# Stacking the queries of the first eight heads by selecting matmuls in place of a trip through DRAM

## The reference

```python
Q = proj(q, Wq, bq); K = proj(k, Wk, bk); V = proj(v, Wv, bv)   # (B, 16, S, 16)
loc_s = einsum('bhnqd,bhnkd->bhnqk', Qb, Kb) * scale            # a block's own 128 keys
out = einsum('bhnqk,bhnkd->bhnqd', softmax(loc_s), Vb)
cross_s = einsum('bhnqd,bhnkd->bhnqk', Qb, Kw) * scale          # keys of blocks n-1, n, n+1
cross_s = where(kmask, cross_s, -inf)
out = out + einsum('bhnqk,bhnkd->bhnqd', softmax(cross_s), Vw)
```

## Time and profile before

| | |
|---|---|
| timed runs, median (lowest to highest) | 917.14 us (916.61 to 918.33) |
| profiled execution, its own time | 918.54 us |
| its span | 916.8 us |
| mean granted clock of PE | 0.926 of full speed |
| PE busy | 820.7 us (90%) |
| DVE, ACT, POOL busy | 401.9, 345.8, 242.9 us |

### The profile page before, as it was taken

The page is one execution under the profiler, slowest core; times in us unless marked ns, Lnnn a source line. Parts: engine busy times, 40 slices in busy tenths (PEclk is TensorE's granted clock), DMA queues, the critical chain, the costliest instruction groups (busy, mean ns, idle before and its releaser), DMA issues. The chain is left out here.

```text
span 916.8 us, 15571 instructions
## 1 busy us (share of the span) xinstructions
PE 820.7 (90%) x5010; PEld 620.5 (68%) x5011; DVE 401.9 (44%) x746; ACT 345.8 (38%) x898; POOL 242.9 (26%) x258
## 2 busy tenths in 40 slices
PE   5689999999999999999399998999999999999930
PEld 4567776767586757757399995766666777666620
DVE  5636585686457644633465542222211222222116
ACT  1121455354434542452354430333333333333313
POOL 5912111141113101200417774111111111111116
PEclk9987999999589957999799999999999999999985
DMA  9952324506050444000561117431111110110034
GB/s 299 173 161 64 56 86 103 96 1 171 16 93 2 113 142 72 1 4 1 193 234 53 58 58 203 133 125 35 29 34 34 34 34 29 34 34 29 23 115 177
DMA packets 56981, 76.83 MB, mean 84 GB/s; under 512 B 15888, under 2 KB 41360, under 8 KB 56048
## 3 DMA queue, kind: packets, MB, share of 16 engines
q1 hardware_dynamic: 53536, 66.99, 27.4%
q0 software_dynamic: 3408, 9.34, 2.9%
HBM read 50.82 MB, written 24.98 MB: 83 GB/s over the span
## 5 line engine op out<-in xcount | busy, mean ns | idle before, releaser
L1678 PE MATMUL ps<-we,xT 128*128 x312 | 142.3, 599 | 1.9 <-issue 1.9
L1698 PE MATMUL ps<-we,hT 128*128 x624 | 141.1, 379 | 2.5 <-ACT hT L794 2.5
L1698 PEld LDWEIGHTS ps<-we,hT 128*128 128x128 f32 x624 | 118.5, 190 | 35.0 <-issue 20.9
L1022 DVE TENSOR_REDUCE mx<-ps 128x4 f32<-128x512 f32 (+1 forms) x128 | 104.1, 821 | 79.4 <-PE ps L1510 77.7
L1226 DVE COPY hp<-ps 128x512 f32<-128x512 f32 x78 | 50.3, 686 | 160.1 <-PE ps L1678 160.1
L794 ACT ACTIVATE hT<-ps,b1T 128x128 f32<-128x128 f32 x312 | 84.7, 382 | 37.2 <-PE ps L1689 37.2
L1678 PEld LDWEIGHTS ps<-we,xT 128*128 128x128 f32 x312 | 56.7, 192 | 59.0 <-issue 58.9
L1510 PE MATMUL ps<-k_stack,q_stack 96*128 96x256 f32 (+1 forms) x256 | 81.9, 410 | 8.2 <-DMA q_stack<-q_rows 5.9
L696 ACT ACTIVATE pT<-ps 128x256 f32<-128x256 f32 x128 | 49.1, 384 | 103.1 <-PE ps L1526 96.3
L590 ACT ACTIVATE xT<-ps 128x256 f32<-128x256 f32 x39 | 14.8, 383 | 180.8 <-PE ps L1661 180.8
L1510 PEld LDWEIGHTS ps<-k_stack,q_stack 96*128 96x128 f32 x256 | 46.0, 224 | 43.9 <-issue 23.8
(11 more groups left out here) (214 smaller groups left out, 1238.2 us busy)
## 6 DMA issues: line engine op xcount, KB each, us to landing
we<-in_w SPq DMA_DIRECT2D x16, 1024.0 KB
k_stack<-k_rows SPq DMA_DIRECT2D x24, 256.0 KB, 4.8
q_stack<-q_rows SPq DMA_DIRECT2D x96, 64.0 KB, 4.8
slot_rows<-attn SPq DMA_DIRECT2D x1, 4992.0 KB, 24.8
xs<-slot_rows SPq DMA_DIRECT2D x39, 128.0 KB, 2.1
k_rows<-k_s SPq DMA_DIRECT2D x16, 256.0 KB, 2.5
q_rows<-q_s SPq DMA_DIRECT2D x16, 256.0 KB, 3.4
yl<-pair_out SPq DMA_DIRECT2D x4, 1024.0 KB, 9.4
```

Source lines behind the costliest of these rows:

```text
L1022: nc.vector.tensor_reduce(mx[:, n, 2 * p:2 * p + 2, r0:r0 + nb], ps[:, 2 * (u % 2):2 * (u % 2) + 2, 0:nb * P].rearrange("p h (b k) -> p h ...
L1678: m = nc.tensor.matmul(ps[:, 2 + c, :], xT[:, q, k, :], w[:, bass.ds(e, 1), k * HID + c * 512:k * HID + (c + 1) * 512].rearrange("p o n -> ...
L1698: m = nc.tensor.matmul(ps[:, 6, 0:D], hT[:, c, :], w[:, bass.ds(e, 1), KD * HID + c * D:KD * HID + (c + 1) * D].rearrange("p o n -> p (o n)"),
```

## The change

The queries of heads 0 to 7 no longer go through DRAM. PE multiplies `q_s[:, 0]` by a selecting matrix `sel` (`q_s` times ones and zeros), two matmuls (high and low part) for each of four pairs of heads, which puts the 96 stacked rows of a pair into PSUM bank `p`. ScalarE (pairs 0 and 2) and VectorE (pairs 1 and 3) copy each bank twice into `q_stack`, once multiplied by `parity[:, 0]` and once by `parity[:, 1]`, per-partition factors of 1 and 0 that clear the other head of the pair. Keys, and queries of heads 8 to 15, go through DRAM as before. The eight matmuls stand ahead of the value matmuls and wait for `cb_out`; the six fillers are gone, while batch 0 keeps its 24 (in bank 5). POOL builds `sel` near its start, VectorE `parity`.

```diff
+        sel = W_s[0][:, 3, :, :, :].rearrange("p l k n -> p (l k n)")[:, 0:PAIRS * 160].rearrange("p (g c) -> p g c", g=PAIRS)
+        parity = sb("parity", [P, 2], F, att)
@@ POOL, behind mask_s
+            nc.gpsimd.memset(sel.bitcast(F), 0.0).then_inc(s["sel_set"], 1)
+            pool.wait_ge(s["sel_set"], 1)
+            for at in (0, 32, 128):
+                nc.gpsimd.tensor_copy(sel[:, :, at:at + 32], ident[:, :].rearrange("p (c g) -> p g c", g=PAIRS))\
+                    .then_inc(s["sel_set"], 1)
@@ ACT, project2, behind projected(3)
+                for p in (0, 2):
+                    act.wait_ge(s["sel_ps"], PAIRS * b + p + 1)
+                    for par in range(2):
+                        last = nc.scalar.activation(q_stack[0:STACK, PAIRS * par + p, :], ps[0:STACK, p, :], ACT.Copy,
+                                                    scale=parity[0:STACK, par:par + 1])
+                    last.then_inc(s["sel_act"], 1)
@@ DVE, start
+            dve.wait_ge(s["consts"], 5)
+            nc.vector.tensor_reduce(parity[:, :], ident[:, :].rearrange("p (k a r) -> p a k r", a=2, r=DH), AXY, ALU.max)\
+                .then_inc(s["parity_set"], 1)
@@ DVE, project2, behind projected(3)
+                for p in (1, 3):
+                    dve.wait_ge(s["sel_ps"], PAIRS * b + p + 1)
+                    for par in range(2):
+                        last = nc.vector.tensor_scalar(q_stack[0:STACK, PAIRS * par + p, :], ps[0:STACK, p, :],
+                                                       parity[0:STACK, par:par + 1], None, ALU.mult)
+                    last.then_inc(s["sel_dve"], 1)
@@ PE, project2
                 projected(3)
+                if c is None:
+                    pe.wait_ge(s["sel_set"], 4)
+                    pe.wait_ge(s["masks"], 1)
+                else:
+                    pe.wait_ge(s["cb_out"], c + 1)
+                pe.wait_ge(s["qk2_lo"], 4 * b + 2)
+                for p in range(PAIRS):
+                    for l in range(2):
+                        m = nc.tensor.matmul(ps[0:STACK, p, :], sel[:, p, 64 * l:64 * l + STACK], q_s[:, 0, l, :],
+                                             start=l == 0, stop=l == 1)
+                    m.then_inc(s["sel_ps"], 1)
                 for i in range(2):
                     pe.wait_ge(s["qk2_lo"], 4 * b + 1 + 2 * i)
                     rows_of(6, c_s, w, 2, "v2_ps", i)
-                if c is not None:
-                    pe.wait_ge(s["cb_out"], c + 1)
-                keep_clock(WARM if c is None else WARM_Q, bank=0)
                 pe.wait_ge(s["qk2_lo"], 4 * b + 4)
+                if c is None:
+                    keep_clock(WARM, bank=5)
@@ PE, half
                         if u == 0:
-                            pe.wait_ge(stacked[ha], 16 * STACK_DMAS * (b + 1))
-                        if u == UNITS // 2:
-                            pe.wait_ge(stacked_late[ha], 16 * LATE_DMAS * (b + 1))
+                            pe.wait_ge(stacked[ha], 16 * (KEY_DMAS + (LATE_DMAS if ha else 0)) * (b + 1))
+                        if ha and u == UNITS // 2:
+                            pe.wait_ge(stacked_late, 16 * LATE_DMAS * (b + 1))
+                        if not ha and u < 2:
+                            pe.wait_ge(s["sel_act"], 2 * b + u + 1)
+                            pe.wait_ge(s["sel_dve"], 2 * b + u + 1)
@@ SP, body of a batch (queries of half 0 and their aways are gone)
                 stack_keys(b, 0)
-                stack_queries(b, 0)
-                rows_away(b, 1, k_rows, k_s, k_away, 1)
-                rows_away(b, 1, q_rows, q_s, q_away, 2)
+                keys_away(b, 1)
+                queries_away(b)
```

More of the change, by code:

```diff
@@ L27 @@
 AX = mybir.AxisListType.X
+AXY = mybir.AxisListType.XY
 P = 128
@@ L55 @@
 WARM = 24
-WARM_Q = 6
 WARM_B = 16
@@ L62 @@
 PAIRS = HALF // 2
-STACK_DMAS = 3 + 2 * 3
+KEY_DMAS = 3
 LATE_DMAS = 2 * 3
+STACK = 96
 def side_blocks(i):
@@ L84, in build @@
         k_rows = nc.dram_tensor("k_rows", (2, 2, P, S), F, kind="Internal").ap()
-        q_rows = nc.dram_tensor("q_rows", (2, 2, P, S), F, kind="Internal").ap()
+        q_rows = nc.dram_tensor("q_rows", (2, P, S), F, kind="Internal").ap()
         pair_out = nc.dram_tensor("pair_out", (2 * T + SLOTS, D), F, kind="Internal").ap()
@@ L213, in build @@
           a_ps a_red aug_step aug_ready augT_ps augT_out b_ps b_exp pv_done oc_out os_out
+          sel_set parity_set sel_ps sel_act sel_dve
           cb_ps w_exp cb_step cb_out v2_ps v2_out at_ps at_hi at_lo w2_ps
@@ L223, in build @@
                                             for n in ("xs_in", "yw_sent", "st_step", "st_sent"))
-        k_away, q_away = ([sem(f"s_{n}_away{h}_{part}") for h in range(2) for part in ("hi", "lo")] for n in "kq")
-        stacked, stacked_late = ([sem(f"s_{n}{h}") for h in range(2)] for n in ("stacked", "stacked_late"))
+        k_away = [sem(f"s_k_away{h}_{part}") for h in range(2) for part in ("hi", "lo")]
+        q_away = [sem(f"s_q_away_{part}") for part in ("hi", "lo")]
+        stacked = [sem(f"s_stacked{h}") for h in range(2)]
+        stacked_late = sem("s_stacked_late")
         yl_in = [sem(f"s_yl_in{b}") for b in range(B)]
@@ L258, in _, with keys_away, queries_away @@
             sp.dma_start(slot_rows[:, D:].rearrange("(i p) d -> p i d", p=P), pad_end[:, :, :]).then_inc(s["pad_out"], 16)
-            def rows_away(b, h, rows, src, away, j):
+            def keys_away(b, h):
                 for part, ready in enumerate(("qk2_hi", "qk2_lo")):
-                    sp.wait_ge(s[ready], 4 * b + 2 * h + j)
-                    sp.dma_start(rows[h, part], src[:, h, part, :].bitcast(F)).then_inc(away[2 * h + part], 16)
+                    sp.wait_ge(s[ready], 4 * b + 2 * h + 1)
+                    sp.dma_start(k_rows[h, part], k_s[:, h, part, :].bitcast(F)).then_inc(k_away[2 * h + part], 16)
+            def queries_away(b):
+                for part, ready in enumerate(("qk2_hi", "qk2_lo")):
+                    sp.wait_ge(s[ready], 4 * b + 4)
+                    sp.dma_start(q_rows[part], q_s[:, 1, part, :].bitcast(F)).then_inc(q_away[part], 16)
             def stack_keys(b, h):
@@ L272, in stack_keys, with stack_queries @@
                                      k_rows[h, part].rearrange("(r g) t -> r g t", g=PAIRS)).then_inc(stacked[h], 16)
-            def stack_queries(b, h):
-                for part_done, g0 in ((stacked, 0), (stacked_late, PAIRS // 2)):
+            def stack_queries(b):
+                for part_done, g0 in ((stacked[1], 0), (stacked_late, PAIRS // 2)):
                     for part, secs in ((0, (0, 1)), (1, (2,))):
-                        sp.wait_ge(q_away[2 * h + part], 16 * b + 16)
+                        sp.wait_ge(q_away[part], 16 * b + 16)
                         for sec in secs:
                             for par in range(2):
-                                r, at = 32 * sec + 16 * par, h * HALF + PAIRS * par + g0
+                                r, at = 32 * sec + 16 * par, HALF + PAIRS * par + g0
                                 sp.dma_start(q_stack[r:r + 16, at:at + PAIRS // 2, :].bitcast(F),
-                                             q_rows[h, part].rearrange("(a r g) t -> a r g t", a=2, g=PAIRS)
-                                             [par][:, g0:g0 + PAIRS // 2, :]).then_inc(part_done[h], 16)
+                                             q_rows[part].rearrange("(a r g) t -> a r g t", a=2, g=PAIRS)
+                                             [par][:, g0:g0 + PAIRS // 2, :]).then_inc(part_done, 16)
             def aug_rows(b, h):
@@ L306, in body @@
                     sp.wait_ge(s["w1_ps"], 2 * B)
+                    sp.wait_ge(s["sel_ps"], PAIRS * B)
                     sp.dma_start(ws[:, 0:KD * HID].rearrange("p (k n) -> p k n", k=KD),
@@ L314, in body @@
                 stack_keys(b, 1)
-                stack_queries(b, 1)
+                stack_queries(b)
                 if not last:
@@ L319, in body @@
                         .then_inc(s["c_raw_in"], 16)
-                    rows_away(b + 1, 0, k_rows, k_s, k_away, 1)
+                    keys_away(b + 1, 0)
                 aug_rows(b, 1)
[L322 to L326, removed]
+            keys_away(0, 0)
             body(0, True, False)
@@ L679, in project2 @@
                 projected(3)
+                if c is None:
+                    act.wait_ge(s["parity_set"], 1)
+                    act.wait_ge(s["masks"], 1)
+                for p in (0, 2):
[4 more added lines that the diff above has]
+                    last.then_inc(s["sel_act"], 1)
                 act.wait_ge(s["ctx_lo"], b + 1)
@@ L1008, in project2 @@
                 projected(3)
+                if c is None:
+                    dve.wait_ge(s["parity_set"], 1)
+                    dve.wait_ge(s["masks"], 1)
+                for p in (1, 3):
[4 more added lines that the diff above has]
+                    last.then_inc(s["sel_dve"], 1)
             def out_cross(c, g):
```

## The result

The changed kernel takes 895.91 us (median of four executions, 895.62 to 896.83) against 917.08 us: a ratio of 0.9769, 95% interval 0.9752 to 0.9786. The forecast was 895 us.

What follows compares the result with a forecast made beforehand. PE was taken as the bound, with DMA waits before the halves of batches 1 to 3 and low clock after two. Terms -1.5 - 1.7 - 0.4 - 12.2 - 9.6 + 1.7 + 1.5 = -22.2 us gave median 895 us, range 889 to 907.

Steps and rivals of the forecast that it cites:

- The waits: PE's waits before the first halves of batches 1, 2, 3: halves start 0.4, 1.5 and 1.7 us earlier.
- sixteen as the prediction says: DMA issues that go from SP: two to DRAM, twelve back, and the waits between; nothing on PE waits for this.
- The step on which 21.8 of 22.2 us rested: First halves of batches 2 and 3: without the waits the low clock goes, saving 12.2 and 9.6 us.
- rival 2: Waits did not lower the clock, the half's own load could; both low stretches stay, 917 us, no change; chance 0.06.
- The 9.6 in place of 12.2: Batch 3's clock gain: 9.6 us with VectorE's `aug` blocked beside POOL's operation, 12.0 without the block.
- the wrong instruction for batch 3: VectorE behind batch 3's half: `aug` L1078 was to be some 2.2 us long there too.
- as a risk: Behind batch 3's half, some 2.7 us of PE idle time; a clock fall there costs about 2 us.
- The start: POOL's added memset and three casts for `sel`, all on the path: +1.5 us, bounds 0.8 and 3.5.
- +3.2: Cost up to batch 0's half: the start's +1.5 us and batch 0's +1.7 us.
- Batch 0's eight matmuls: Selecting matmuls added ahead while the 24 fillers stay: +1.9 us, less 0.2 us of former wait, +1.7 us.

Runs made afterwards that it cites:

- all three edits: Changed kernel without batch 0's 24 fillers, with POOL's last-batch v_aug write held behind aug, and sel built late: 885.14 us; run once more, 884.79 us.

## Why the prediction was right

In the profiled executions the time fell by 22.9 us (918.54 to 895.62) for a forecast of 22.2, between the medians by 21.2.

*The waits.* Batches 1 to 3 saved 0.7, 1.4 and, with the clock, 13.8 us; the copies and keys were in time. ScalarE's masked copies took 0.68 us each, VectorE's 0.74 where I had taken 0.68, and the keys of batch 2 landed within 4.7 us of issue. VectorE's four copies of batch 2, after, end at 225.1, 0.7 us ahead of the half:

```profile
222.41 2.71 DVE L1041 TENSOR_SCALAR q_stack<-ps,parity 96x512 fp32r<-96x512 f32 x4
```

The DMA issues that went from SP are fourteen per batch (two writes, twelve reads), not sixteen as the prediction says; nothing hung on the number.

*The clock.* The step on which 21.8 of 22.2 us rested held in both batches, to 0.1 us. For batches 2 and 3, rival 2 (the half's own load) falls by the runs with more fillers and with late copies. The rule of the Trainium skill, page "TensorE: Matmul & The Clock Gate", section "Why this matters for your kernels", warns only of gaps longer than these. The measurement decides: shorter ones do harm here, since idle times of 2.03, 2.11, 2.26 (twice) and 2.28 us each brought the low clock. The length alone does not say what follows: 1.41 us did nothing in the profiled execution, and 2.49 us once brought about 3.4 us at the low clock, at a price of 0.8 us.

Nor does a fall need such a wait. In batch 0 the first half starts 0 to 0.23 us behind fillers or value matmuls, and the clock falls inside it in every profile. PE is busy for 2.9 of the first 4 us below, waiting for VectorE in between (after; columns as in the earlier trace rows):

```profile
68.00:72.00 4.00, 2.87 (x14) 1.67 (x12) 3.05 (x5) 0.00 (x0) 3.92 (x3) 0.96 0.01 2
72.00:76.00 4.00, 3.64 (x9) 2.37 (x10) 3.46 (x5) 0.00 (x0) 1.40 (x1) 0.50 0.00 0
76.00:80.00 4.00, 3.74 (x10) 2.11 (x9) 3.56 (x5) 0.00 (x0) 0.00 (x0) 0.50 0.00 0
```

So in batch 0 the half's own work, with its short waits for VectorE, lowers the clock; in batches 1 to 3 it does not.

*The price of staying low.* The profiles show eight halves of batches 1 to 3 in which the clock fell: two in the kernel before, three with no fillers, three with late copies. In seven of them it stayed at 0.50 to about the half's end, and they took 9.6 to 13.6 us longer: that is why a wait of 2 us costs 12. In the eighth it came back within the half, after some 3.4 us. What brings it back is not shown. In batch 2 before, it rose at 258.0, 1.0 us into the projections behind the half. In batch 3 before, where no projections follow, it rose at about 353.5, with the half's last value matmuls just done:

```profile
352.00:354.00 2.00, 2.00 (x28) 1.10 (x20) 1.45 (x8) 0.55 (x2) 0.29 (x1) 0.61 0.00 0
354.00:356.00 2.00, 1.64 (x16) 1.53 (x15) 0.36 (x1) 0.94 (x3) 2.00 (x1) 1.00 0.04 8
```

*Batch 3.* The 9.6 in place of 12.2 rested on VectorE being blocked by POOL. It was, and the run without it gave the 2.2 us back. I had named the wrong instruction for batch 3: the cast, not the subtraction behind it, was caught (in batches 1 and 2 after it was the subtraction, 2.37 and 2.28 us). The Trainium skill, page "SBUF — State Buffer", section "Who interferes with whom", lists casts among what can contend with GpSimd; the cast's 2.34 us agree. The fall of the clock behind it, which I had priced at about 2 us as a risk, came and cost 1.5 us.

*The start.* POOL's memset and casts took more than I had summed:

```profile
14.80 0.63 POOL L421 MEMSET w_s<- 128x640 f32 x1
15.50 1.11 POOL L424 CAST w_s<-ident 128x128 fp32r<-128x128 f32 x3
16.54 0.32 POOL L426 MEMSET attn<- 128x256 f32 x1
```

From 14.80 to 16.54 that is 1.74 us for a forecast of 1.5; the stride cost 0.1 us a cast. PE began only 0.55 us later (49.16 for 48.61), since POOL was 1.2 us earlier in this execution (its memset of `ident` started at 13.18, for 14.36). That +2.4 came out in place of +3.2 was luck of the profiled executions: in the six profiles with `sel` built early PE begins at 49.16 to 50.50, mean 49.72, in the three on the old path at 47.84 to 48.61, mean 48.23, which are the 1.5 us of the forecast. The run with `sel` built late gave 1.5 us. Batch 0's eight matmuls cost what the others do.

*What I missed* was not in the time but in the reading: the 24 fillers ahead of batch 0 most likely had the same reason as the six, and I kept them as given. Their 5.47 us were worth more than the 3.7 us by which the halves of batches 1 to 3 start earlier (0.7, 1.4 and, without the clock, 1.6).

## What to carry to other kernels

Price a wait on PE by what runs behind it, not by its length: look in the granted clock for a fall just after it, and for how long the work that follows leaves it low. Before rebuilding a data path to remove such a wait, fill it with enough useless matmuls; if that gives the gain, the path was not the problem. When a wait is removed, the fillers that guarded it turn into work on the path and should go with it, in every place.

## What the runs showed of the hardware

Waits of much the same length ended differently. In the profiles 2.49 us cost 0.8 us of slower work, and 2.03 to 2.28 us cost 9.6 to 13.6. The kernel before shows such a spread from one execution to the next: of its ten executions in the last comparison one took 905.64 us at a mean clock of 0.942, three 929.4 to 932.3 us at 0.907 to 0.912, and six 916.7 to 919.3 us at 0.921 to 0.925. These are steps of 12 to 13 us, the price of one half; that one, two or three halves ran at the low clock is inferred from the times and clocks, since only one execution near 917 us was profiled.

The versions with no wait ahead of the halves of batches 1 to 3 are steadier. Of the 38 executions of these eight kernels all but two lay within 3.2 us of the others of the same kernel. The two are 904.96 us (POOL's write held back, mean clock 0.911) and 1915.89 us (all three edits); neither is explained.
